# Sums over the pixels of one sample moved from TensorE's one-column matmuls to GpSimd's adds, and a product with the identity turned into a transposition

## The reference, cut to what matters

```python
out = relu(bn(einsum('oc,bchw->bohw', w_conv1, x)))
d = relu(bn(einsum('oc,bchw->bohw', w_dr, out) + b_dr))      # 128 rows x 3136 pixels
xf = d.reshape(B, C2, M)
xc = xf - mean(xf, axis=2)
cov = einsum('bim,bjm->bij', xc, xc) / M                     # 128 x 128
r = einsum('cjh,bch->bcj', w_row, bn(cov)).reshape(B, 4 * C2) + b_row
att = sigmoid(einsum('oc,bc->bo', w_fc, r) + b_fc)
return x * att
```

## Time and profile before

| | |
|---|---|
| time of three runs | 1863.67 us median (1863.25 to 1864.05) |
| time of the profiled execution | 1863.55 us |
| its span in the trace | 1861.5 us |
| PE busy | 1695.1 us (91%) |
| DVE busy | 1571.5 us (84%) |
| ACT busy | 1481.1 us (80%) |
| POOL busy | 460.5 us (25%) |

### The profile page before, as it was taken

The page is one execution under the profiler, slowest core; times in us unless marked ns, Lnnn a source line. Parts: engine busy times, 40 slices in busy tenths (PEclk is TensorE's granted clock), DMA queues, the critical chain, the costliest instruction groups (busy, mean ns, idle before and its releaser), DMA issues.

```text
span 1861.5 us, 40140 instructions
## 1 busy us (share of the span) xinstructions
PE 1695.1 (91%) x13394; PEld 1315.0 (71%) x13394; DVE 1571.5 (84%) x2887; ACT 1481.1 (80%) x2257; POOL 460.5 (25%) x136
## 2 busy tenths in 40 slices
PE   7999999999993235588999999999999999999999
PEld 8999999999992012366576666666666766767665
DVE  6888888888887889788988888888888888888886
ACT  7777777777778997788878788888788787887886
POOL 7888888888880000000000000000000000000000
PEclk9999999999996557699999999999999999999999
DMA  9998998998999999405546455455464464554535
GB/s 334 374 376 303 373 373 307 373 367 312 372 356 402 430 430 429 196 1 220 174 162 236 164 186 209 164 211 186 156 234 168 169 230 158 196 199 166 214 140 208
DMA packets 141137, 477.38 MB, mean 256 GB/s; under 512 B 10657, under 2 KB 33569, under 8 KB 126369
## 3 DMA queue, kind: packets, MB, share of 16 engines
q1 hardware_dynamic: 141088, 476.75, 69.4%
HBM read 284.04 MB, written 192.68 MB: 256 GB/s over the span
## 4 chain that ended last, share of the span: by engine, by line
PE 51%; DVE 1%; issue 0%; ACT 0%; DVEq 0%; ACTq 0%
PE y_ps L1067 16%; PE z_ps L1090 16%; PE d_ps L1018 12%; PE cov_ps L1000 5%; PE ch_ps L1078 1%; PE ch_ps L1031 0%; PE ch_ps L1030 0%; DVE hl L1249 0%; PE y_ps L1047 0%; DVE q L1227 0%; DVE g L1261 0%; PE cov_ps L1003 0%; DVE gg L1271 0%; PE z_ps L1047 0%; DVE p_res L1351 0%
## 5 line engine op out<-in xcount | busy, mean ns | idle before, releaser
L310 POOL TENSOR_TENSOR xl<-early,xh 128x1568 fp32r<-128x1568 f32 x128 | 459.6, 3591 | 96.6 <-ACT xh L265 96.6
L1090 PE MATMUL z_ps<-qr,wh 128*128 128x512 f16 (+1 forms) x880 | 307.4, 352 | 1.3 <-ACT h L1160 1.3
L1090 PE MATMUL z_ps<-qr,wl 128*128 128x512 f16 (+1 forms) x880 | 307.7, 353 | 0.0
L1249 DVE TENSOR_TENSOR hl<-h,hh 128x1024 f16<-128x1024 f32 (+2 forms) x224 | 243.8, 1089 | 75.0 <-ACT hh L1165 74.8
L265 ACT ACTIVATE xh<-early 128x1568 fp32r<-128x1568 f32 x128 | 194.2, 1517 | 139.4 <-PE pp L327 139.3
L1018 PE MATMUL d_ps<-vh,hh 128*128 128x128 f16 x1600 | 280.1, 219 | 4.7 <-DVE hl L1249 4.6
L1018 PE MATMUL d_ps<-vl,hh 128*128 128x128 f16 x1600 | 279.8, 219 | 0.0
L1018 PE MATMUL d_ps<-vh,hl 128*128 128x128 f16 x1600 | 279.8, 219 | 0.0
L327 PE MATMUL pp<-xh,uh 128*128 128x392 f32 x1024 | 267.2, 342 | 9.3 <-ACT xh L265 9.3
L1160 ACT ACTIVATE h<-z_ps,sb_h 128x512 f32<-128x512 f32 (+1 forms) x442 | 260.2, 625 | 19.4 <-PE z_ps L1090 11.6
L1067 PE MATMUL y_ps<-qr,udh 128*128 128x512 f16 (+2 forms) x784 | 274.1, 353 | 0.0
(11 more groups left out here) (211 smaller groups left out, 3014.9 us busy)
## 6 DMA issues: line engine op xcount, KB each, us to landing
early<-in_x_dram SPq DMA_DIRECT2D x128, 784.0 KB, 6.8
out_dram<-p_res SPq DMA_DIRECT2D x30, 3136.0 KB, 10.2
early<-p_scratch SPq DMA_DIRECT2D x42, 1568.0 KB, 12.7
p_res<-p_scratch SPq DMA_DIRECT2D x112, 512.0 KB, 4.3
p_scratch<-early SPq DMA_DIRECT2D x56, 784.0 KB, 7.7
p_scratch<-late SPq DMA_DIRECT2D x56, 784.0 KB, 7.8
p_res<-p_scratch SPq DMA_DIRECT2D x56, 384.0 KB, 3.2
late_tile<-p_scratch SPq DMA_DIRECT2D x13, 1568.0 KB, 12.8
```

What stands on the lines that cost most here:

```text
L310: nc.gpsimd.tensor_tensor(xl[:, k % 2], xs[:, k], xh[:, k % 2].bitcast(F32), ALU.subtract).then_inc(split_done, 1)
L1090: last = nc.tensor.matmul(z_bank(r2, a, s)[:, m, 0:w], part[:, k, m * P:(m + 1) * P], qr[:, a, k, columns(s)], start=k == 0 and part is wh ...
L1249: nc.vector.tensor_tensor(hl[:, par, :, 0:w], h32[:, par, :, 0:w], hh[:, par, :, 0:w], ALU.subtract).then_inc(h_split, 1)
```

## The change

The column of ones goes from `gg`, and with it the one-column matmuls: there is one matmul of 256 columns for each tile. GpSimd gets a program in the third block. For each chunk it adds `g32` to `tile_sums` (tile by tile and channel by channel); behind the sixth chunk it folds the four tiles into two and these into `pixel_sums`, and the three tiles of the last chunk are added to `pixel_sums` one by one. In the steps that have a y it starts behind the step's conversion (`q_converted`). `spread` then makes three things: the transpose of `hl_sb` by a transposition, the sums in every row as the product of all ones with `pixel_sums`, and the sums down the partitions as the product of `pixel_sums` with a column of ones. `rectified_g` waits until GpSimd has read `g32`. The memset of `gg` (128 x 2064 fp16) becomes one of `zeros` (128 x 512 fp32).

```diff
-            gg = cb("gg", [P, 2, G, 2 * P + 2], F16)
+            gg = cb("gg", [P, 2, G, 2 * P], F16)
+            tile_sums = cb("tile_sums", [P, G, P])
+            pixel_sums = cb("pixel_sums", [P, P])
+            zeros = cb("zeros", [P, G, P])
...
-                            nc.tensor.matmul(cov_ps[:, 0:2 * P + 1], gg[0:q, par, t, 0:P],
-                                             gg[0:q, par, t, 0:2 * P + 1], start=c == 0 and t == 0,
-                                             stop=False)
-                            last = nc.tensor.matmul(cov_ps[:, 2 * P:2 * P + 1], gg[0:q, par, t, P:2 * P],
-                                                    gg[0:q, par, t, 2 * P:2 * P + 1], start=False, stop=end)
+                            last = nc.tensor.matmul(cov_ps[:, 0:2 * P], gg[0:q, par, t, 0:P], gg[0:q, par, t],
+                                                    start=c == 0 and t == 0, stop=end)
...
-                        pe.wait_ge(diag_done, n)
                         pe.wait_ge(hl_copied, n)
+                        pe.wait_ge(pixels_summed, n)
 
                         wait_from(pe, att_done, n - 1)
-                        nc.tensor.matmul(ch_ps[:, 0:P], hl_sb[:], ident[:], start=True, stop=True)
-                        nc.tensor.matmul(ch_ps[:, P:2 * P], ones[:], dg[:], start=True,
+                        nc.tensor.transpose(ch_ps[:, 0:P], hl_sb[:], ident[:])
+                        nc.tensor.matmul(ch_ps[:, P:2 * P], ones[:], pixel_sums[:], start=True, stop=True)
+                        nc.tensor.matmul(ch_ps[:, 2 * P + K:2 * P + K + 1], pixel_sums[:], ones[:, 0:1], start=True,
                                          stop=True).then_inc(spread_done, 1)
...
                         wait_from(dve, g_split, g - 1)
+                        wait_from(dve, g_added, g - 1)
                         nc.vector.scalar_tensor_tensor(out=g32[0:dq, 0:dt], in0=d_ps[0:dq, 1 - par, 0:dt],
...
                         nc.vector.tensor_copy(hl_sb[:], cov_ps[:, P:2 * P]).then_inc(hl_copied, 1)
-                        nc.vector.tensor_scalar(dg[:], ident[:], cov_ps[:, 2 * P:2 * P + 1], -1.0 / M, ALU.mult,
-                                                ALU.mult).then_inc(diag_done, 1)
-                        nc.vector.tensor_copy(s_sb[:], cov_ps[:, 2 * P:2 * P + 1])
...
                         dve.wait_ge(spread_done, n)
+                        nc.vector.tensor_scalar(s_sb[:], ch_ps[:, 2 * P + K:2 * P + K + 1], -1.0 / M, None,
+                                                ALU.mult).then_inc(s_read, 1)
                         dve.wait_ge(cov_read, n)
-                        nc.vector.scalar_tensor_tensor(out=a_sb[:], in0=ch_ps[:, P:2 * P], scalar=s_sb[:, 0:1],
+                        nc.vector.tensor_tensor(a_sb[:], ch_ps[:, 0:P], a_sb[:],
+                                                ALU.add).then_inc(cov_centred, 1)
+                        dve.wait_ge(s_read, n)
+                        dve.wait_ge(cov_centred, 2 * n - 1)
+                        nc.vector.scalar_tensor_tensor(out=cov_sb[:], in0=ch_ps[:, P:2 * P], scalar=s_sb[:, 0:1],
                                                        in1=a_sb[:], op0=ALU.mult,
                                                        op1=ALU.add).then_inc(cov_centred, 1)
-                        dve.wait_ge(cov_centred, 2 * n - 1)
-                        nc.vector.tensor_tensor(cov_sb[:], ch_ps[:, 0:P], a_sb[:],
-                                                ALU.add).then_inc(cov_centred, 1)
...
+            @block.gpsimd
+            def _(pool):
+                pool.wait_ge(zeros_set, 1)
+
+                def phase(r2, a):
+                    n = 2 * r2 + a
+                    for s in range(CH):
+                        if not has(r2, a, s, 2):
+                            continue
+                        g, c = first_chunk(r2, a) + s, (s - 2) % CH
+                        full, rest = widths[c] // P, widths[c] % P
+                        pool.wait_ge(d_read, g - 1)
+                        if has(r2, a, s, -LEAD) and not has_no_y(r2, a, s):
+                            pool.wait_ge(q_converted, g + 1)
+                        if c == 0:
+                            nc.gpsimd.tensor_tensor(tile_sums[:], zeros[:], g32[:], ALU.add).then_inc(g_added, 1)
+                        elif c < CH - 1:
+
+                            pool.wait_ge(g_added, g - 2)
+                            nc.gpsimd.tensor_tensor(tile_sums[:, 0:full], tile_sums[:, 0:full], g32[:, 0:full],
+                                                    ALU.add).then_inc(g_added, 1)
+                        if c == CH - 2:
+
+                            pool.wait_ge(g_added, g - 1)
+                            nc.gpsimd.tensor_tensor(tile_sums[:, 0:2], tile_sums[:, 0:2], tile_sums[:, 2:4],
+                                                    ALU.add).then_inc(tiles_folded, 1)
+
+                            pool.wait_ge(tiles_folded, FOLDS * (n - 1) + 1)
+                            wait_from(pool, spread_done, n - 1)
+                            nc.gpsimd.tensor_tensor(pixel_sums[:], tile_sums[:, 0], tile_sums[:, 1],
+                                                    ALU.add).then_inc(tiles_folded, 1)
+                        if c == CH - 1:
+                            for t in range(full):
+                                pool.wait_ge(tiles_folded, FOLDS * (n - 1) + 2 + t)
+                                nc.gpsimd.tensor_tensor(pixel_sums[:], pixel_sums[:], g32[:, t],
+                                                        ALU.add).then_inc(tiles_folded, 1)
+                            pool.wait_ge(tiles_folded, FOLDS * n)
+                            nc.gpsimd.tensor_tensor(pixel_sums[0:rest], pixel_sums[0:rest], g32[0:rest, full],
+                                                    ALU.add).then_inc(g_added, 1)
+                            pool.wait_ge(g_added, g - 1)
+                            pool.sem_inc(pixels_summed, 1)
+
+                phases(pool, phase)
```

More of the change, by code:

```diff
@@ L800, in layer_kernel @@
         mean_q, constant_done, bias_done = sem("mean_q"), sem("constant_done"), sem("bias_done")
-        constant_read, gg_set = sem("constant_read"), sem("gg_set")
+        constant_read, zeros_set = sem("constant_read"), sem("zeros_set")
         q_converted, z_read = sem("q_converted"), sem("z_read")
@@ L804, in layer_kernel @@
         gh_done, g_split, cov_done, cov_read = sem("gh_done"), sem("g_split"), sem("cov_done"), sem("cov_read")
-        hl_copied, diag_done, spread_done = sem("hl_copied"), sem("diag_done"), sem("spread_done")
+        hl_copied, spread_done, s_read = sem("hl_copied"), sem("spread_done"), sem("s_read")
+        g_added, tiles_folded, pixels_summed = sem("g_added"), sem("tiles_folded"), sem("pixels_summed")
         cov_centred, r_summed, r_done = sem("cov_centred"), sem("r_summed"), sem("r_done")
@@ L828, in layer_kernel @@
             s_sb = cb("s_sb", [P, 1])
-            dg = cb("dg", [P, P])
             cov_sb = cb("cov_sb", [P, P])
@@ L918, in final @@
                 return isinstance(o, int) and o >= FINAL
+            FOLDS = 2 + widths[CH - 1] // P
+            assert G == 4 and widths[CH - 1] % P > 0
             final_ps = [y_ps, z_ps, d_ps.rearrange("p m g c -> p m (g c)")]
@@ L1147, in phase @@
                             act.wait_ge(d_read, g - 1)
-                            if isinstance(r2, int) and r2 == 0:
-                                act.wait_ge(gg_set, 1)
                             wait_from(act, cov_done, g - 3)
@@ L1240, in _ @@
                 nc.vector.tensor_tensor(sb_h[:], bh, cov_ps[:, 0:K], ALU.subtract).then_inc(bias_done, 1)
-                nc.vector.memset(gg[:], 1.0).then_inc(gg_set, 1)
+                nc.vector.memset(zeros[:], 0.0).then_inc(zeros_set, 1)
                 def low_half_of_h(r2, a, s):
```

## The result

The changed kernel takes 1954.29 us (median of four runs, 1952.85 to 1954.89) against 1863.86 us of the kernel before beside it: a ratio of 1.048, 95% interval 1.0465 to 1.0501. It is slower by 90 us; 1953 us was forecast. The profiled execution took 1954.67 us with a span of 1952.7 us.

A forecast was written before the change was run, and what follows sets the result against it. TensorE was taken as the loop's bound, with DVE becoming it through exclusion by GpSimd's adds: 1863.55 + 82 (loop) + 8 (samples ahead) = 1953.5, forecast as 1953 us, with an overall range of 1842 to 1990 us.

The forecast's parts named there:

- TensorE sets the pace before, DVE is close behind: Third block's loop before the change: TensorE bounds it at 34.0 us per sample; DVE without its waits needs 30.7 us.
- TensorE gains 0.75 us on the covariance and `spread` costs 0.07: TensorE, per sample: 25 one-column matmuls of 0.03 us go, `spread` costs 0.07 us more; need falls to 33.3 us.
- The adds' length: GpSimd in the third block: 2.29 ns an element, 8.2 us per sample; the other bound, with fixed time, 10.8 us.
- The two engines exclude each other, and DVE pays: SBUF reads: GpSimd's adds and DVE's two-input or double-pace instructions exclude each other; whichever waits, DVE pays.
- 6.4 us blocked, against 3.3 us of DVE's slack, so that DVE is full: DVE in the loop: 30.6 plus 6.4 us blocked makes 37.0 us per sample, above TensorE's 33.3, so DVE becomes the bound.
- The way on which the loss comes out: `g_added` wait of `rectified_g`: DVE's next step, ACT's high half of g and TensorE's covariance stand behind it; 2.9 us.
- 82 us in the loop and 8 us ahead of it: Loop: 3.0 us more for each of 27.5 samples; 4.6 samples without y ahead: nothing to 15 us, 8 taken.
- The last three adds are ready for `spread`: Step 1 to `spread`: 3.3 us for 0.9 us of adds and three hand-overs, costed at nothing more.
- The first rival: Adds run freely beside DVE and TensorE stays the bound: 33.3 us per sample, 1843.5 us; chance 0.33.
- The mechanism's edge: DVE's break-even in the loop: 3.4 us blocked per sample (0.3 more or less) changes nothing, 1864 us; chance 0.07.

The follow-up runs named there:

- length against number: Changed kernel with the adds of the first six chunks cut to two tiles in place of four or three, as many instructions: 1911.01 us, ratio 1.0258.
- the early start: Changed kernel without GpSimd's wait for the conversion, so its add starts as soon as g is rectified: 1952.42 us, ratio 1.0483.
- two buffers: Changed kernel with g32 in two buffers alternating by step, so rectified g waits only for the add of the step before: 1929.74 us, ratio 1.035.
- the run with writes: Changed kernel with each GpSimd add replaced by a write-only memset of three times as many elements, behind the same waits: 1884.99 us, ratio 1.0114.

## Why the prediction was right, point by point

- **TensorE sets the pace before, DVE is close behind**: right. With the adds left out TensorE is the bound again.
- **TensorE gains 0.75 us on the covariance and `spread` costs 0.07**: the first right (33.70 us less 0.51 us of waits in the chain of the run without adds, against 34.05 less 0.12, is 0.74 us); `spread` costs 0.01 (0.45 against 0.44 us).
- **The adds' length**, 1.17 us for 512 elements taken, 1.37 as the other bound: beside an instruction that does not exclude them they take 1.26 us (above); the small ones take 0.45 us (the row of L1408), not 0.29. By these two and the 0.99 us between them for 384 elements, the adds need about 9.6 us per sample (an estimate). The 8.2 us taken were on the low side, and the 9.6 lie inside the bounds.
- **The two engines exclude each other, and DVE pays**: right, and shown from four sides: reads against writes, length against number, another place, and the kernel before with the adds alone. The row that the prediction held beside it, 3.55 against 3.59 us, could not test this, as DVE read only PSUM there. The rule of the Trainium skill in "SBUF — State Buffer", section "Who interferes with whom", agrees in all its parts that this case touches: two inputs from SBUF against a GpSimd read (0.69 us from the add's end to the end of the 640-element subtraction), no exclusion by a GpSimd write (825 ns beside the memsets), exclusion of a double-pace instruction by either, and none of one with a single SBUF operand (0.68 us).
- **6.4 us blocked, against 3.3 us of DVE's slack, so that DVE is full**: the difference was right, each term too large by 2.4 us. Compared with the run without adds, DVE's instructions are longer by 0.9 us (low half of h on 768 elements, twice), 0.72 (640), 0.10 (1024, four times), 1.02 (weight product) and 0.29 (four products), and rectified g waits 0.97 us: 4.0 us. DVE's waits for ACT are 3.1 us per sample in that run ((58.8 + 15.0) us in 800) and still 2.4 us in the changed kernel ((37.7 + 13.8) us in 800). 4.0 - 0.7 = 3.3 us is what lies between their periods (33.70 and 36.97). Against the kernel before, 4.0 - 0.9 is the same 3.1 us as 6.4 - 3.3. That the two errors are of one size has a reason: the part of an add that lies beneath a wait of DVE for ACT blocks nothing and leaves the wait, and the prediction booked it both as blocked and as slack used up. In the sample of the timeline above (1401 to 1438 us), 2.2 us of adds lie so. But "DVE is full" was wrong for the changed kernel: in steps 4, 5 and 0 the low half of h still waits for hh, which hangs on a z that TensorE makes late. Only the early start shows a DVE with next to no wait, 760.28 of 800 us busy, at about the same pace.
- **The way on which the loss comes out**, the `g_added` wait of rectified g: that wait is a third of it. With two buffers 0.98 us per sample go; 2.3 us (35.99 - 33.70) come out without it, by DVE's own instructions being late. TensorE's waits stand before the covariance and y, not before d.
- **82 us in the loop and 8 us ahead of it**: about 76 and 15. The loss ahead is at the top of the bounds that were given (nothing to 15 us), the loss in the loop is smaller since its last samples lose less. The two errors cancel. That the forecast of 1953 us lies within 1.3 us of the measured time is in part luck.
- **The last three adds are ready for `spread`**: right in the changed kernel, where TensorE does not wait at `spread`; it holds only for this place of the adds, as the run with the adds behind the low half of h shows.
- **The first rival at 1843.5 us**: its price was wrong. Without any interference the kernel takes 1852.91 us, since 0.4 of the 0.74 us that TensorE gains per sample go into waits of y and the covariance for ACT and DVE. Had the adds been free, the forecast for that case would have been 9 us too low.
- **The mechanism's edge**: the run with writes shows that a hand-over of 0.35 us and one held-up instruction already turn 11 us of gain into 21 us of loss.

## What to carry to other kernels

An idle engine is not free: count the time of its reading instructions into the budget of the engine that they exclude; here GpSimd's 8 to 10 us per sample had to fit into DVE's 3.3 us of waits and beside its instructions that read PSUM. The place mattered (35.40 to 36.97 us per sample in the complete versions of the change), but none of those tried was good enough. And watch what a later place does to the engine that waits for the result. When the bound engine is relieved, look up which engine it will wait for next before booking the whole saving: 0.4 of 0.7 us went there. And time the parts of a compound change one by one: a loss of 101 us hid a transposition that gains 3 us by itself.

## What the runs showed of the hardware

- A GpSimd add of 512 fp32 elements takes 1.26 us when it starts beside a DVE instruction with one SBUF and one PSUM operand, a small one of 128 elements 0.45 us: about 0.18 us fixed and 2.1 ns per element ((1.26 - 0.45) / 384).
- A GpSimd memset of 1536 elements takes 1.38 us and leaves DVE's two-input subtraction at 825 ns, but stretches a double-pace instruction from 347 to 1186 ns.
- The exclusion works both ways, for the length of the instruction, in the order of arrival, and the recorded duration contains the time held up (an add of 512 elements is recorded with 1.65 us in the changed kernel): the adds of step 1 wait for the low half of h (1.85 us for two), and the one of step 6 makes it wait (1547 ns for 825).
- An fp32 transposition of 128 x 128 follows at 0.11 us, half of the product with the identity, and TensorE shows one instruction in place of two.
